# Routing two of four token blocks of a mixture through sorted blocks of 128 rows

## What is computed

```python
sg = einsum('td,sdh->tsh', xf, sw1); su = einsum('td,sdh->tsh', xf, sw3)
shared_out = einsum('tsh,shd->td', silu(sg) * su, sw2)
logits = xf @ router_w.T + experts_bias
rw, sel = top_k(logits, 2);  rw = softmax(rw)
cw = (one_hot(sel, E) * rw[..., None]).sum(axis=1)
eo = silu(einsum('td,edh->teh', xf, w1)) * einsum('td,edh->teh', xf, w3)
moe_out = einsum('te,teh,ehd->td', cw, eo, w2)
x = x + 0.5 * (moe_out + shared_out)
```

## Time and profile before

| | |
|---|---|
| median of three runs | 1084.19 us |
| the profiled execution | 1078.49 us |
| its span | 1076.8 us |
| granted TensorE clock, mean | 0.925 |
| TensorE busy | 933.8 us, 87% |
| VectorE busy | 708.1 us, 66% |
| ScalarE busy | 619.6 us, 58% |
| GpSimd busy | 337.8 us, 31% |

### The profile page before, as it was taken

One profiled execution on the slowest core, in us unless ns is written; L12 is line 12 of the kernel. 1 busy time (PEld: TensorE's weight loads), 2 busy tenths in 40 slices (PEclk: granted clock), 3 DMA queues, 4 the chain that ended last, 5 costly groups with the idle time before them and its releaser, 6 DMA issues.

```text
span 1076.8 us, 13026 instructions
## 1 busy us (share of the span) xinstructions
PE 933.8 (87%) x4507; PEld 628.2 (58%) x4507; DVE 708.1 (66%) x1413; ACT 619.6 (58%) x1003; POOL 337.8 (31%) x249
## 2 busy tenths in 40 slices
PE   6899999579999999879999997799967777777997
PEld 4678887123333333337788876488644545455886
DVE  3978887467778777646788886744276556547532
ACT  6555555268888888863555555544554545455454
POOL 1597777000000000001677775201201221123200
PEclk8999999689999999997999998699988778888999
DMA  5125110000000000003311110200000000001001
GB/s 172 43 79 159 66 62 27 0 1 0 1 1 1 0 1 0 1 0 118 76 64 64 64 50 16 63 21 2 1 0 3 4 2 2 4 1 39 1 2 40
DMA packets 30743, 33.64 MB, mean 31 GB/s; under 512 B 2062, under 2 KB 19798, under 8 KB 30678
## 3 DMA queue, kind: packets, MB, share of 16 engines
q1 hardware_dynamic: 30678, 32.81, 9.9%
HBM read 31.36 MB, written 1.18 MB: 30 GB/s over the span
## 4 chain that ended last, share of the span: by engine, by line
PE 61%; DVE 19%; ACT 11%; issue 4%; POOL 3%; DMA 0%; ACTq 0%; SPq 0%; DVEq 0%; POOLq 0%
PE ps L128 10%; PE ps L129 10%; PE ps L130 10%; PE ps L750 5%; PE ps L862 4%; PE ps L744 2%; ACT ex L1485 2%; PE ps L955 2%; PE ps L728 2%; ACT L1374 2%; POOL fl L2155 2%; DVE smax L2034 1%; PE ps L891 1%; PE ps L964 1%; PE ps L736 1%
## 5 line engine op out<-in xcount | busy, mean ns | idle before, releaser
L2155 POOL TENSOR_TENSOR fl<-fp,fh 128x512 fp32r<-128x512 f32 x144 | 223.5, 1568 | 126.3 <-ACT fh L1280 126.0
L1271 ACT ACTIVATE fs<-ps 128x512 f32<-128x512 f32 x144 | 86.2, 599 | 114.6 <-PE ps L130 114.4
L1743 DVE TENSOR_TENSOR fp<-fp,cwb 128x512 f32<-128x512 f32 x128 | 141.2, 1103 | 14.0 <-DVE fp L1736 0.9
L1736 DVE TENSOR_TENSOR fp<-fs,ps 128x512 f32<-128x512 f32 x144 | 98.2, 682 | 40.7 <-ACT fs L1271 40.1
L128 PE MATMUL ps<-z_hi,w_hi 128*128 128x512 f32 x288 | 117.0, 406 | 3.3 <-DVE fp L1736 3.3
L129 PE MATMUL ps<-z_lo,w_hi 128*128 128x512 f32 x288 | 116.6, 405 | 0.0
L130 PE MATMUL ps<-z_hi,w_lo 128*128 128x512 f32 x288 | 115.0, 399 | 0.0
L1280 ACT CAST fh<-fp 128x512 fp32r<-128x512 f32 x144 | 88.8, 617 | 36.8 <-DVE fp L1743 32.6
L2219 POOL TENSOR_TENSOR ln_sq<-ln_rs 128x512 f32<-128x512 f32 x20 | 21.1, 1056 | 272.4 <-ACT ln_rs L1337 272.4
L2212 POOL TENSOR_SCALAR_AFFINE_SELECT ex<-ex 128x1024 f32<-128x1024 f32 (+1 forms) x24 | 33.4, 1403 | 152.4 <-ACT ex L1485 152.4
L2034 DVE TENSOR_REDUCE smax<-ps 128x8 f32<-128x2048 f32 (+1 forms) x24 | 55.0, 2291 | 38.8 <-PE ps L969 31.9
...
## 6 DMA issues: line engine op xcount, KB each, us to landing
...
```

The source lines that it names most:

```text
L1271: act.activation(fs[:, n % 2, :], ps[:, n % 2, :], ACT.Silu).then_inc(silu_done, 1)
L1736: dve.tensor_tensor(f, fs[:, n % 2, :], ps[:, 2 + n % 2, :], ALU.mult).then_inc(prod_done, 1)
L1743: dve.tensor_tensor(f, f, cwb[:, x % CW_RING, :], ALU.mult).then_inc(weighed, 1)
L2155: pool.tensor_tensor(fl[:, n % RING0, :], fp[:, n % RING0, :], f32(fh[:, n % RING0, :]), ALU.subtract).then_inc(flo_done, 1)
```

## The change

Token blocks 0 and 1 stay dense. Token blocks 2 and 3 keep their shared units, but their routed units are replaced. 1024 tokens with two experts each are 2048 rows; they are sorted by expert, each expert's rows padded to whole blocks of 128, which makes at most 16 + 7 = 23 blocks (`BLOCKS0`). All 23 are always computed. The steps:

- After units 1 and 2 TensorE turns the tokens of blocks 2 and 3 (high and low parts) to rows, 16 transposes; ScalarE copies them and SyncE stores them in DRAM (`z_rows`, 1024 rows of 1 KB).
- TensorE makes each token's rank within its expert with 9 short bf16 products (`ranks`, after unit 6), VectorE the places, and one-hot tables of block and row (units 8 to 17), TensorE from them the table of which token fills which row with 16 short products (`table`, after unit 19), VectorE the indices `take` and `give` and the `owner` of each block (units 20 and 21). The shared part of blocks 2 and 3 is added to `xr` at units 14 and 15.
- GpSimd stops its subtractions after unit 21 (`LOW0`), and does then only indirect DMAs, a gather of 128 rows and a scatter of 128 rows for each block, with four buffers for the rows and four for the results. The subtraction of units 22 to 39 goes to VectorE (`low`).
- A block: `rows_in`, two transposes; ScalarE copies them (`xs`); `rows_up`, three products with the rows as stationary operand and 512 columns of weights, those of the expert whose number TensorE's queue reads from `owner`; `rows_gate` on ScalarE, `rows_product` on VectorE on 128x256; `hidden_turned`, two transposes; `hidden_high` on ScalarE, `hidden_low` on VectorE; `rows_down`, six products of 128 columns into one sum; `rows_out` on VectorE; the scatter to `y_rows` in DRAM.
- The first 16 blocks are interleaved with the dense units 24 to 39, one each; the other seven run by themselves (`LATE0`). Then SyncE loads the results of both choices of each token (`load_sums`, four transfers of 256 KB), VectorE multiplies them with their weights (`weigh_rows`), TensorE adds and turns them back (`summed`, 16 products with the identity), and VectorE adds them to `xr` (`add_summed`).
- In call 1 the centring, variances and scores of L1 ffn for blocks 0 and 1 stand after the last block; the weighing stands ahead of the top-8 rounds and `add_summed` after the first of them.

The core of the diff (the weights' layout changes from one tensor each for high and low parts to one for both, which is left out, as are the bodies of the routing steps):

```diff
-ALL0 = NTB * UNITS0
 SHARED0 = NTB * HT0
+DENSE0 = 2
+DT = DENSE0 * TPB
+ALL0 = SHARED0 + DENSE0 * EXP * HT0
 CW_RING = 4
-ROUTED0 = NTB * EXP
+ROUTED0 = DENSE0 * EXP
+PLAIN0 = SHARED0 + EXP * HT0
+LOW0 = PLAIN0 - 2
+ST = TILES - DT
+SROWS = ST * P
+COLS0 = 2 * ST
+BLOCKS0 = 2 * ST + EXP - 1
+MIXED0 = EXP * HT0
+XG_RING, Y_RING = 4, 4
+CHUNKS = W0 // P
...
+        def gu_bank(b):
+            return 4 if b >= 8 and b % 2 == 0 else 7
+        def x_bank(b):
+            return b % 2 if b > MIXED0 else 6
+        def t_bank(b):
+            return 3 if b > MIXED0 and b % 2 == 1 else 6
...
+            def load_sums(call):
+                for r in range(2):
+                    sp.wait_ge(y_out[r], 16 * scattered(call + 1, r))
+                for tb in range(NTB - DENSE0):
+                    for k in range(2):
+                        lo = k * SROWS + tb * TB
+                        sp.dma_start(yr[:, tb, k, :, :], y_dram[lo:lo + TB, :].rearrange("(q p) d -> p q d", p=P)).then_inc(yr_in, 16)
...
+                def rows_in(b):
+                    pe.wait_ge(xg_in[b % XG_RING], 16 * gathered_in(call, b))
+                    if b == 0:
+                        pe.wait_ge(route_vector, TV(call, "owners"))
+                    elif b == 1:
+                        pe.wait_ge(rows_scalar, RS(call, "in", 0))
+                    elif b <= MIXED0:
+                        pe.wait_ge(rows_vector, RV(call, "low", b - 2))
+                    elif b == MIXED0 + 1:
+                        pe.wait_ge(prod_done, U + ALL0)
+                    elif b >= MIXED0 + 3:
+                        pe.wait_ge(rows_scalar, RS(call, "in", b - 2))
+                    for half in range(2):
+                        ins = pe.transpose(ps[:, x_bank(b), half * P:(half + 1) * P], xg[:, b % XG_RING, half * P:(half + 1) * P], ident[:])
+                    ins.then_inc(rows_matmul, 1)
+                def rows_up(b):
+                    pe.wait_ge(rows_scalar, RS(call, "in", b))
+                    if b >= 1:
+                        pe.wait_ge(rows_vector, RV(call, "product", max(b - 1 - (gu_bank(b) != gu_bank(b - 1)), 0)))
+                    if b == 8:
+                        pe.wait_ge(a0_in if call == 0 else ln_in, 1 if call == 0 else NTB * LN_FFN1 + 1)
+                    e = pe.value_load(owner[0:1, b:b + 1], min_val=1, max_val=EXP)
+                    hi, lo = (w0[:, bass.ds(e, 1), 0:2 * HT0, half, :].rearrange("p a c n -> p (a c) n") for half in range(2))
+                    out = ps[:, gu_bank(b), :]
+                    x_hi, x_lo = xs[:, b % 2, 0:P], xs[:, b % 2, P:2 * P]
+                    pe.matmul(out, x_hi, hi, start=True, stop=False)
+                    pe.matmul(out, x_hi, lo, start=False, stop=False)
+                    pe.matmul(out, x_lo, hi, start=False, stop=True).then_inc(rows_matmul, 1)
+                    return e
+                def hidden_turned(b):
+                    pe.wait_ge(rows_vector, RV(call, "product", b))
+                    if b == 0:
+                        pe.wait_ge(rows_scalar, RS(call, "in", 1))
+                    elif b <= MIXED0:
+                        pe.wait_ge(rows_vector, RV(call, "out", b - 1))
+                    elif b >= MIXED0 + 2:
+                        pe.wait_ge(rows_vector, RV(call, "out", b - 2))
+                    for t in range(HT0):
+                        ins = pe.transpose(ps[:, t_bank(b), t * P:(t + 1) * P], sf[:, b % 2, t * P:(t + 1) * P], ident[:])
+                    ins.then_inc(rows_matmul, 1)
+                def rows_down(b, e):
+                    pe.wait_ge(rows_vector, RV(call, "low", b))
+                    if b + 2 <= MIXED0:
+                        pe.wait_ge(rows_scalar, RS(call, "in", b + 2))
+                    out = ps[:, t_bank(b), 2 * P:3 * P]
+                    for t in range(HT0):
+                        hi, lo = (w0[:, bass.ds(e, 1), 2 * HT0 + t, half, :].rearrange("p a n -> p (a n)") for half in range(2))
+                        h = slice(t * P, (t + 1) * P)
+                        pe.matmul(out, sh_hi[:, b % 2, h], hi, start=(t == 0), stop=False)
+                        pe.matmul(out, sh_hi[:, b % 2, h], lo, start=False, stop=False)
+                        ins = pe.matmul(out, sh_lo[:, b % 2, h], hi, start=False, stop=(t == HT0 - 1))
+                    ins.then_inc(rows_matmul, 1)
...
+                for n in range(1, PLAIN0):
                     up(n)
                     if n >= LAG0:
                         down(n - LAG0)
...
+                    if n in (1, 2):
+                        tokens_turned(2 * n - 2)
+                        tokens_turned(2 * n - 1)
                     if n == LAG0 + 1:
                         weights()
...
+                    if n == LAG0 + 2:
+                        ranks()
+                    if n == PLAIN0 - 5:
+                        table()
+                owners = {}
+                rows_in(0)
+                for b in range(MIXED0):
+                    n = PLAIN0 + b
+                    rows_in(b + 1)
+                    owners[b] = rows_up(b)
+                    if b >= 1:
+                        rows_down(b - 1, owners[b - 1])
+                    up(n)
+                    hidden_turned(b)
+                    down(n - LAG0)
+                for b in LATE0:
+                    owners[b] = rows_up(b)
+                    if b + 1 < BLOCKS0:
+                        rows_in(b + 1)
+                    if b == MIXED0:
+                        rows_down(b - 1, owners[b - 1])
+                    elif b > MIXED0 + 1:
+                        rows_down(b - 2, owners[b - 2])
+                    if b - MIXED0 < LAG0:
+                        down(ALL0 - LAG0 + b - MIXED0)
+                    if b > MIXED0:
+                        hidden_turned(b - 1)
+                hidden_turned(BLOCKS0 - 1)
+                for b in range(BLOCKS0 - 2, BLOCKS0):
+                    rows_down(b, owners[b])
+                if call == 0:
+                    for tb in range(NTB - DENSE0):
+                        summed(tb)
+                else:
+                    ln_centre(LN_FFN1, 0)
+                    ln_centre(LN_FFN1, 1)
+                    pe.wait_ge(lxc_copied, later(LN_FFN1, 1))
+                    ln_variance(LN_FFN1, 0)
+                    ln_variance(LN_FFN1, 1)
+                    scores(LN_FFN1, 0)
+                    scores(LN_FFN1, 1)
                     rows_turned(0, LN_FFN1, 0)
                     rows_turned(0, LN_FFN1, 1)
+                    for tb in range(NTB - DENSE0):
+                        summed(tb)
+                    chances(0, 0)
...
+                def rows_gate(b):
+                    act.wait_ge(rows_matmul, RM(call, "up", b))
+                    if b >= 2:
+                        act.wait_ge(rows_matmul, RM(call, "turn", b - 2))
+                    act.activation(sf[:, b % 2, :], ps[:, gu_bank(b), 0:H0], ACT.Silu).then_inc(rows_scalar, 1)
...
+                rows_in(0)
+                for b in range(MIXED0):
+                    rows_in(b + 1)
+                    rows_gate(b)
+                    high(PLAIN0 + b - 1)
+                    gate(PLAIN0 + b)
+                    hidden_high(b)
                 high(ALL0 - 1)
...
+                def rows_product(b):
+                    dve.wait_ge(rows_scalar, RS(call, "gate", b))
+                    dve.tensor_tensor(sf[:, b % 2, :], sf[:, b % 2, :], ps[:, gu_bank(b), H0:], ALU.mult).then_inc(rows_vector, 1)
+                def hidden_low(b):
+                    dve.wait_ge(rows_scalar, RS(call, "high", b))
+                    dve.tensor_tensor(sh_lo[:, b % 2, :], ps[:, t_bank(b), 0:2 * P], f32(sh_hi[:, b % 2, :]), ALU.subtract).then_inc(rows_vector, 1)
+                def rows_out(b):
+                    dve.wait_ge(rows_matmul, RM(call, "down", b))
+                    if b >= Y_RING:
+                        dve.wait_ge(y_out[b % 2], 16 * scattered(call, b % 2, b))
+                    dve.tensor_copy(ys[:, b % Y_RING, :], ps[:, t_bank(b), 2 * P:3 * P]).then_inc(rows_vector, 1)
+                def weigh_rows(tb):
+                    dve.wait_ge(yr_in, 64 * (call + 1))
+                    t = DT + tb * TPB
+                    for k in range(2):
+                        ins = dve.tensor_tensor(yr[:, tb, k], yr[:, tb, k], pr[:, k, t:t + TPB, None].broadcast_to([P, TPB, P]), ALU.mult)
+                        if k == 0:
+                            own.did(ins)
+                    ins.then_inc(yw_done, 1)
...
+                    if n == 8:
+                        ranked()
+                    if n == 9:
+                        slots()
+                    if n == 10:
+                        slot_parts()
+                    if n in (11, 12, 13):
+                        block_hot(13 - n)
+                    if n == 14:
+                        add_shared(2)
+                    if n == 15:
+                        add_shared(3)
```

(61 more changed lines are left out.)

347 lines of the change are left out of this document (284 added, 63 removed).

## The result

The changed kernel takes 1162.68 us (median; 1158.39 to 1165.03) where the kernel before takes 1084.26 beside it: 1.071 times as long, 95% interval 1.066 to 1.076. The profiled execution took 1158.39 us, its span is 1156.5 us; before, the span was 1076.8. The forecast was 1140 in a range of 1104 to 1178, so side and range held. It was 22.7 us too low.

The account below looks back on a forecast made before the run. It took TensorE to bound the kernel; call 0 +31.3 us and call 1 +27.7, together +59, on 1078.5 gave 1137.5, and 2.5 more for timed runs gave 1140 us, 5% slower, range 1104 to 1178.

Parts of the forecast that it names:

- (b): Dense units 0 to 23: TensorE's additions 4.4 us plus VectorE's overflow and contention, together 9.5 us a call, between 5 and 17.
- Contention with GpSimd: Dense units 8 to 21: VectorE's small instructions slowed beside GpSimd, 0 to 8 us, taken as 0.6.
- The stand: First block: TensorE stands 3 us until GpSimd has finished its last subtraction and the first gather has landed.
- The mixed round: Sixteen rounds: TensorE work 4.02 us, 1.05 waiting on hidden_low's chain, 0.5 register read; 5.57 each, 89.1 a call.
- The read's price: Ahead of rows_up: TensorE's register read of the expert number exposed for 0 to 1.07 us, taken as 0.5.
- Rival 3: Register read in every block costs all of 1.07 us or more, giving 1166 us; chance 10%.
- Rival 2: GpSimd's gather and scatter take 4.3 us a block and bound the seven late blocks, giving 1170 us; chance 15%.
- Late blocks: Seven blocks after the mixed rounds: 2.42 us each with the register read, no other wait, 17.0 us a call.
- The end of call 0: Scatter, loads, weighing, sums and last addition before the attention's first product: 13.3 us, where it was 6.4 before.
- that sign: Call 0, after some 13 us without TensorE between last down and attention: clock 0.5 would show the forecast right.
- The end of call 1: From the last down to the top-k, with centring, variances, scores and weighing: 17.4 us, where it was 12.0 before.
- Rival 1: All waits vanish and the round is TensorE's 4.02 us, giving 1063 us, faster; chance 5%, with 8% for between.

Follow-up runs that it names:

- the order experiment: Changed kernel with each mixed round's block transposes, high half and low half put ahead of the dense unit's own products, silu and product: 1130.59 us.
- The order and the early read together: Both edits (block steps ahead of the dense unit's, expert number read a round early) were run with three more on the changed kernel: 1115.61 us.
- a filled end: On top of five edits to the changed kernel, call 0's first attention period put ahead of weighing and summing blocks 2 and 3: 1102.91 us.

## Why the prediction was right, and where it was off

It had the chain and the bound of each stage that the traces show, and most sizes a little too small: the sum was 20.9 us too small for the profiled execution. The rounds have 8.4 of this, the end of call 0 4.3, the stands 3.5, the dense stretches 2.1, and 4.1 lie behind call 1, where the forecast had no term. By its own steps:

- *The dense stretch* (b). 9.5 a call forecast, 10.5 and 10.6 measured. The 10.8 us of waiting for VectorE's product are not this term alone, as the 3.1 us of the kernel before show. With every wait of TensorE in the stretch counted, they grew from 5.9 to 12.5 us in call 0 and from 1.1 to 7.1 in call 1, 6.6 and 6.0 where 5.1 was forecast; TensorE's own additions (transposes 1.56 and 0.79, ranks 0.25, table 0.56 us) are 3.2 in place of 4.4. That VectorE sets the stretch is shown twice: more table work made it longer, less made it shorter. "Contention with GpSimd adds 0 to 8; I take 0.6" was the weakest step and came out right by chance: in call 0 the tables met GpSimd at 2.17 and 1.89 us, in call 1 they did not (0.53 and 0.32), and yet both calls were late by the same; what takes the place of the tables in call 1 stays open (2.5 us of VectorE's waiting for the spread weights are part of it in the groups of 540 to 625 us).
- *The stand.* 3 us forecast, 4.8 and 4.7 measured: 3.47 until the first rows and 1.3 more until the second. The forecast also left out the clock behind a stand: in round 0 the products are 0.43 us apart and the round takes 6.98 us.
- *The mixed round.* 5.57 forecast, 5.73 measured in steady rounds (105.05, 110.79, 116.52): the stand 0.93 for 1.05, the read 0.47 for 0.5 and, where ScalarE's copy adds to it, 0.62. TensorE's own work in it is 4.33 us for 4.02 (5.87 - 0.62 - 0.92, from 163.67 to 169.54): ahead of a wait a product counts with its whole 0.40 us, and the sum had the pitch of products in a row; the stand and the read were put slightly too high and hid half of that. One round of call 0 took 6.92 (128.02 to 134.94), with the clock at 0.50 from 131 to 133 us, and the last round of call 1 has 0.50 from 697 to 700 us. 16 rounds came to 93.3 for 89.1, the largest miss of the sum, 4.2 us in each call; round 0 and the slow one have 2.4 us of this in call 0. That the chain of sh_lo sets the round is shown by the order experiment, which took 32 us.
- *The read's price.* 0.5 was taken between 0 and 1.07; the trace has 0.47, and moving it took 19.6 us in all. Rival 3 falls.
- *Rival 2, GpSimd's queue.* An indirect transfer holds GpSimd for 0.97 us (median), 0.30 lie between two, and 2.5 us a block is under every round. The stands for rows in late blocks are 0.24 us in call 0 and 1.09 in call 1, and VectorE waited once in each call for a scatter to land (0.61 and 0.60 us). It falls, but it is near: most late blocks take 2.5 to 3 us.
- *Late blocks.* 21.9 and 22.1 for 23.3 and 22.9.
- *The end of call 0,* the term furthest off in one place: 17.6 for 13.3. The loads were right (216.24 to 222.01, 5.8 us) and so was the weighing (2.50 for 2.8). The sums were put at 1.2 us here, though the forecast's own count of TensorE's work had 2. The trace has 32 passes for the 16 products, and behind ten us without work each takes 0.21: 6.68 us at a clock of 0.56. The forecast had said that the clock would be 0.5 behind the stand, and did not carry it into the price; that sign held for the sums, but not for the attention's first product, which took 1.10 us at 1.00.
- *The end of call 1.* 17.6 for 17.4; there the sums are 5.37 us and lie mostly beside the layer norm.
- *Rival 1, faster.* It needed all waits to go. The order and the early read together took most of those in the rounds, and with a filled end the kernel is still 20.7 us behind. That agrees with the forecast's remark that a round of 4.02 alone would not turn the sign, but the shortest round reached was 4.57, so the remark itself was not tried. Where those 20.7 lie was not measured by a kernel of its own; what is left in view are 9 us a call in the dense stretch, the stand of 3.2 and 1.7 us, seven blocks with no dense unit beside them, and the end of call 1.
